# Delta rule in a two-layer kernel: the recurrence parts of the first two chunks move one slot earlier

## The reference, cut to what matters

```python
h = rmsnorm(layernorm(x))
q, k, v = (causal_conv_silu(h @ W, conv) for W, conv in ...)   # width 4 along the tokens
q, k = l2norm(q) * Kd ** -0.5, l2norm(k)
g = -exp(A_log) * softplus(h @ Wa + dt_bias);  beta = sigmoid(h @ Wb)
for each token:                                # S is 64 x 128 a head
    S = S * exp(g)
    delta = (v - k @ S) * beta
    S = S + outer(k, delta)
    o = q @ S
o = rmsnorm(o) * silu(h @ Wg)
x = x + o @ Wo
out = gelu(layernorm(x) @ W2 + b2) + x
```

## Time and profile before

| | |
|---|---|
| median of 3 runs | 4597.69 us (4597.64 to 4602.04) |
| the profiled execution | 4567.66 us, of it 4565.7 us span |
| TensorE busy | 3937.4 us (86%) |
| VectorE, ScalarE, GpSimd busy | 54%, 44%, 24% |
| delta rule, about | 2220 to 3960 us of the span |
| mean granted TensorE clock over the span | 0.927 |

### The profile page before, as it was taken

The page is one execution under the profiler, slowest core; times in us unless marked ns, Lnnn a source line. Parts: engine busy times, 40 slices in busy tenths (PEclk is TensorE's granted clock), DMA queues, the critical chain, the costliest instruction groups (busy, mean ns, idle before and its releaser), DMA issues. The chain is left out here.

```text
span 4565.7 us, 72621 instructions
## 1 busy us (share of the span) xinstructions
PE 3937.4 (86%) x23860; PEld 3048.4 (67%) x23860; DVE 2462.8 (54%) x5456; ACT 1990.0 (44%) x4069; POOL 1089.9 (24%) x1689
## 2 busy tenths in 40 slices
PE   5888788598999999993788888888888888769998
PEld 3555555377888888881577666666767677646666
DVE  7888888552222222224577767777777776421111
ACT  5655655111222222212466666666666666432222
POOL 0111111102222222212333433333333332200000
PEclk8888889799999999996799999999999999879999
DMA  1010010245555555552111111111111110011111
GB/s 34 29 42 28 28 42 20 78 133 180 184 184 184 184 184 184 184 169 71 37 38 43 44 37 42 43 42 43 42 43 43 42 43 24 20 51 55 55 55 46
DMA packets 220428, 345.93 MB, mean 76 GB/s; under 512 B 99956, under 2 KB 171380, under 8 KB 201972
## 3 DMA queue, kind: packets, MB, share of 16 engines
q1 hardware_dynamic: 196404, 271.69, 18.7%
q0 software_dynamic: 23760, 71.07, 4.9%
HBM read 275.56 MB, written 67.63 MB: 75 GB/s over the span
## 5 line engine op out<-in xcount | busy, mean ns | idle before, releaser
L525 ACT ACTIVATE moe_rel<-moe_fc 128x512 f32<-128x512 f32 x284 | 169.6, 597 | 799.6 <-PE moe_fc L490 799.6
L490 PE MATMUL moe_fc<-moe_xT,moe_win 128*128 128x256 f32 x2272 | 505.0, 381 | 1.5 <-issue 0.8
L501 PE MATMUL moe_o<-moe_wout,moe_hT 128*128 128x256 f32 x2272 | 502.0, 379 | 0.0
L490 PEld LDWEIGHTS moe_fc<-moe_xT,moe_win 128*128 128x128 f32 x2272 | 433.5, 191 | 61.5 <-issue 2.1
L501 PEld LDWEIGHTS moe_o<-moe_wout,moe_hT 128*128 128x128 f32 x2272 | 426.3, 190 | 55.1
L549 DVE TENSOR_TENSOR moe_hT<-moe_rel 128x512 f32<-128x512 f32 x284 | 196.7, 693 | 362.0 <-ACT moe_rel L525 362.0
L1777 DVE SCALAR_TENSOR_TENSOR gdr_y<-gdr_bank,gdr_cw,gdr_y 128x511 f32<-128x511 f32 (+2 forms) x384 | 287.5, 749 | 81.2 <-ACT gdr_y L2045 61.5
L2252 PE MATMUL gdr_bank<-gdr_hT,gdr_wqkv 128*128 128x512 f32 x512 | 260.4, 633 | 41.3 <-ACT gdr_qk L2060 24.7
L558 DVE COPY moe_osb<-moe_o 128x512 f32<-128x512 f32 x71 | 49.1, 692 | 424.9 <-PE moe_o L501 424.9
L723 DVE TENSOR_TENSOR ffn_z<-ffn_o,ffn_xres 128x512 f32<-128x512 f32 x32 | 20.6, 686 | 381.2 <-PE ffn_o L690 381.2
L690 PE MATMUL ffn_o<-ffn_wout,ffn_hT 128*128 128x256 f32 x1024 | 225.2, 381 | 0.0
(11 more groups left out here) (391 smaller groups left out, 8398.3 us busy)
## 6 DMA issues: line engine op xcount, KB each, us to landing
moe_win<-in_moe_w SPq DMA_DIRECT2D x71, 1024.0 KB, 8.0
moe_wout<-in_moe_w SPq DMA_DIRECT2D x71, 1024.0 KB, 5.2
slots_out<-moe_osb POOLq DMA_DIRECT2D x71, 256.0 KB, 7.5
ffn_xin<-mixed_rows SPq DMA_DIRECT2D x17, 512.0 KB, 3.8
gla_xp<-in_xT_rows SPq DMA_DIRECT2D x16, 512.0 KB, 4.7
gla_xres<-in_x_rows SPq DMA_DIRECT2D x16, 512.0 KB, 3.9
token_rows<-gla_x POOLq DMA_DIRECT2D x16, 512.0 KB, 3.4
rt_W<-in_fc_b SPq DMA_DIRECT2D x32, 256.0 KB, 3.3
```

The costliest lines, as they stand in the source:

```text
L490: ins = nc.tensor.matmul(fc_ps[j][:, m % 2, :], win[u][:, c, m * P:(m + 1) * P], xT[:, c, :], start=(c == 0), stop=(c == DT - 1))
L501: ins = nc.tensor.matmul(o_ps[u][:, t, :], hT[u][:, k, t * P:(t + 1) * P], wout[u][:, k, :], start=(k == 0), stop=(k == FT - 1))
L525: nc.scalar.activation(rel[:, j, :, :], fc_ps[j][:], ACT.Relu).then_inc(relu_done, 1)
```

## The change

Every part of chunks 0 and 1 goes one slot forward: slots 8 to 13 in place of 9 to 14, on all three engines. The squares of their outputs on ScalarE (`squares`, L2117) go from slots 12 and 15 to 11 and 14. On TensorE the block of `chunk(0, ...)` and `chunk(1, ...)` is put behind the key products in the code, so that in slot 8 the key products of the second pair come first; the wait for the scans (`DT`) moves to slot 8 with it. Nothing is added or taken away.

```diff
 CHUNK_AT = {0: (2, 0), 1: (2, 1), 2: (2, 2), 3: (3, 0), 4: (3, 1), 5: (3, 2),
-            9: (0, 0), 10: (0, 1), 11: (0, 2), 12: (1, 0), 13: (1, 1), 14: (1, 2)}
+            8: (0, 0), 9: (0, 1), 10: (0, 2), 11: (1, 0), 12: (1, 1), 13: (1, 2)}
...
-                        if here and slot in (12, 15):
-                            squares(0 if slot == 12 else 1, b)
+                        if here and slot in (11, 14):
+                            squares(0 if slot == 11 else 1, b)
...
-                        if t is not None and t < 2 and here:
-                            if slot == 9:
-                                pe.wait_ge(s["DT"], b * TT + TT)
-                            chunk(t, part, b, u)
                         if here and lv < 0:
                             if slot == 0 and past:
                                 pe.wait_ge(s["Uf"], b * TT)
                             if slot == 0 and end:
                                 pe.wait_ge(s["yb"], (b - 1) * 2)
                             key_products(pair, b, u)
+                        if t is not None and t < 2 and here:
+                            if slot == 8:
+                                pe.wait_ge(s["DT"], b * TT + TT)
+                            chunk(t, part, b, u)
```

## The result

The changed kernel took **4694.61 us** (median of 4 runs, 4673.76 to 4707.93) against 4599.86 (4 runs, 4597.64 to 4604.44) for the kernel before: ratio **1.0195 [1.0165, 1.0224]**, slower. The forecast was 4600 with a range up to 4628, so it was wrong. The same change was run twice more beside the kernel before: 1.0154 [1.0125, 1.0183] and 1.0145 [1.0118, 1.0172]. The cost of the change is therefore about 1.5% (61 to 68 us); what the first comparison had beyond that is told apart further down.

What follows compares the result with a forecast made beforehand. TensorE sets the pace through its own work, stalls and the clock lost after stalls. Per period -1.7 + 1.8 = +0.1, about +2 over 14 periods, so 4570, plus 30 us profile-to-median difference: 4600 us, range 4573 to 4628.

Steps and rivals of the forecast that it cites:

- the walk: One period followed on TensorE, VectorE and ScalarE from slot 8 to slot 14: -1.7 us if the clock stays high.
- the XT wait: Slot 12: TensorE's stall for the XT copies shrinks from 2.42 us to 0.3, as the squares went to slot 11.
- The last step: After the start of `first_half(5, 3)` in slot 14, old and new order are the same and TensorE is dense.
- the mark: Start of `first_half(5, 3)` in slot 14, at 2973.08 before and 2971.4 predicted; if it moves, the period moves.
- two signs of being wrong: Prediction would be wrong if `mix_out(0)` is slow in most periods, or if `reach` does not wait.
- The mean clock of the stretch: Delta rule's mean clock, 0.94 before: above 0.96 was to show the clock holds, at or below 0.94 the rates last.
- What the clock takes back: Low clock after the three new stalls in slots 9, 10/11 and 13: together 1.8 us a period.
- stall for R: Slot 9: TensorE waits 3.2 us for VectorE's R; clock drops in 3 of 4 periods, 1.3 each, 1.0 on average.
- rates' stall: Slots 10 and 11: TensorE waits 2.0 us for the softplus chain; clock drops 1 in 4 at 1.2, 0.3.
- stall for U's copy: Slot 13, before `first_half(4, 3)`: stall grows from 1.2 to 2.5 us; clock drops 1 in 2 at 1.0, 0.5.
- every new stall drops the clock: Rival: all three new stalls punished every time, 2.1 + 1.7 + 1.0 - 1.7 = +3.1 a period, 4641 us; chance 0.06.
- rates last: Rival: `rates(1)` behind the state's update on VectorE, `mix_out(0)` not faster; +2.0 a period, 4626 us; chance 0.27.

Runs made afterwards that it cites:

- rates_first: The changed kernel with VectorE's rates and scaled keys of slot 10 put ahead of the state's update: 4647.45 us, ratio 1.0153 to the kernel before.
- warm_half: The changed kernel with four spare unread matmuls in slot 9's wait for R and four in slot 13's wait for the U copy: 4597.52 us, 1.0042.
- chunk1_back: The changed kernel with chunk 1 back in slots 12 to 14 and its squares in 15, only chunk 0 moved: 4658.63 us, 1.0175.
- r_behind: The changed kernel with TensorE's chunk(0,1) of slot 9 put behind the rates and the first three turn_o: 4621.14 us, 1.0097.
- the third series: Runs on one chip with spare unread matmuls: three of the changed kernel (1.0123, 1.0183, 1.0187), one of the old kernel with chunk 0's squares in slot 11 (0.9938).
- the fifth: Series on another chip: the old kernel with chunk 0's squares at the end of slot 11 (4579.53 us, 0.9953), and the old kernel unaltered (4604.3, 1.0).
- before_2: The old kernel once more, unaltered: 4604.3 us, ratio 1.0.
- gather_late: The changed kernel with GpSimd's gathers for sequence b+2 held until the period's last merge is done: 4674.38 us, 1.0211.
- squares_back: The changed kernel with ScalarE's squares left in slots 12 and 15 as before: 4624.84 us, 1.0109.

## Why the prediction was wrong

**What held.** Each stall and each chain of the walk, in place and size: R 3.2 us (3.2 predicted), the rates 1.9 (2.0), U's copy 2.4 (2.5), `mix_out(0)` at the high clock (in 32 of 36 periods of the three profiles of the change), the XT wait down to 0.6 (0.3). Only the wait ahead of `mix_out(0)` is 1.0 and not 1.5, since TensorE comes late to it. From the start of `mix_out(0)` to that of `mix_out(1)` it took 10.4 us (10.1), from the end of `mix_out(1)` to `first_half(4, 3)` 8.2 (8.3). The last step, that behind the mark nothing changes, holds in the repeats: 16.4 to 16.5 us from the mark to the next period, 16.3 before. Neither of the two signs of being wrong that the prediction named came: `mix_out(0)` is fast in most periods, and `reach` waits. The mean clock of the stretch, at or below 0.94, was to point at the rates; it points at drops of the clock elsewhere.

**What failed is the step "What the clock takes back".** It took 1.8 us a period and should have taken 6.6 (the mark at 50.2, walked 43.6):

| term | priced | measured | from |
|---|---|---|---|
| stall for R | 1.0 (3 in 4 at 1.3) | 2.8 | `mix_out(0)` at 17.2, walked 14.4 |
| rates' stall | 0.3 (1 in 4 at 1.2) | 0.5 | rest of the 3.3 by which `mix_out(1)` ends late |
| stall for U's copy | 0.5 (1 in 2 at 1.0) | 3.4 | 10.5 from `first_half(4, 3)` to the mark, walked 7.1 |
| TensorE's lateness hidden in slots 12 and 13 | 0 | -0.1 | `first_half(4, 3)` 3.2 late behind 3.3 |

The difference of 4.8 a period, 14 times, is 67 us. Three errors are in it.

- I read single old stalls, one with a drop and one without, as a coin, while the drop came in nearly every period: `mix_out(0)` started at 16.5 or later in 23 of 24 periods of the two repeats, and all 24 were slow at the end. The profile of the kernel before had shares to read it from. In each of its 12 periods the stall of 3.16 us is followed by a slow `mix_out(0)` (5.2 to 6.6 us), and in 8 of the 12 the stall of 2.42 us is followed by a first product of level 4 (L2375) of 1.8 us in place of 1.0. I had followed one period, which had the longest `mix_out(0)` but one; from the mean old mark, 45.1, the walk gains 1.5 us and not 1.7.
- I priced a drop by the instruction that happened to stand behind the old stall (2.7 for one `mix_out`), but the low clock goes on through whatever follows, 7 to 9 us of dense work in the period shown.
- I let ScalarE's copies hide half of it, though their inputs, the `turn_o` results, come from the slowed TensorE: `rates` and three `turn_o` took 3.0 us longer than priced (3.42 and 2.80 against 1.85 and 1.4), and 2.8 of it arrived at `mix_out(0)`.

The third, largest term had been bounded at 1.5. The rival "every new stall drops the clock" had the mechanism nearly right, at a chance of 0.06. But its prices (2.1, 1.7 and 1.0) were too small where it mattered and came to +3.1 a period and 4641, where +5.1 was measured; by the prediction's own upper bounds (2.7, 1.7 and 1.5) it would have been +4.2. Its price for the rates' stall was too large: only in 6 of the 24 periods of the repeats is `mix_out(0)` or `mix_out(1)` at the low clock.

The Trainium skill (TensorE: Matmul & The Clock Gate, Part 1, on what is actually happening) was weighed there for a free-running window, from which the prediction drew that the same stall is punished or not by where it falls. The traces agree that equal stalls fare differently: in `rates_first` a wait of 2.25 us at one place of the period is followed by the low clock in some periods and by the high one in others. But the shares can't be taken from that, nor from the length of the stall. The wait for U's copy was punished in 24 of 24 periods of the repeats, in 10 of 12 of the change's first profile (waits of 1.7 and 1.8 us in the other two) and in 6 of 12 of `rates_first`. In `rates_first` the outcome goes with what TensorE did before, the length of `mix_out(1)`, but what decides it in a given period no run here tests.

That the clock is the cause, and not merely beside it, is shown by warm_half: with the stalls filled, the walked times come at both places, 14.4 to the start of `mix_out(0)` and 7.1 from `first_half(4, 3)` to the mark. 42 of the 61 us come back; the other 18 or 19 are still lost, most of them ahead of `first_half(4, 3)`, and for those the cause is read from the low clock in the rows there, not tested. That chunk 0's move brings in the stalls for R and for the rates is shown by chunk1_back; that the stall ahead of `rates` costs time, by r_behind.

**The rival "rates last"** had its mechanism wrong: `mix_out(0)` was fast, and taking the wait away (rates_first) gave nothing, since S came last in its place. That the time came out slower, as it said, is luck.

**The rest of the 95 us.** The first profile of the change has something that the repeats lack: VectorE and ScalarE start late in slot 15, and the profile names no instruction that held them:

```profile
3034.23 0.59 ACT L2141 COPY gdr_U<-gdr_bank 128x512 f32<-128x512 f32 x1 [8.12 <-remote]
...
3034.23 0.69 DVE L1932 TENSOR_TENSOR gdr_x<-gdr_bank,gdr_b 128x512 f32<-128x512 f32 x1 [1.68 <-remote]
```

```profile
3035.36 0.87 PE L2389 MATMUL gdr_bank<-gdr_U,gdr_Y 128*64 128x64 f32 x6 [5.13 <-ACT gdr_Y L2143]
```

From the mark to the next period it took 19.2 us, 16.4 in the repeats. This isn't of the change. Waits of this kind are in every trace taken where the old kernel's median was near 4600 (the first comparison, the third series and the fifth), in the old kernel's own too, profiled at 4603.92 (before_2):

```profile
DVE gdr_U L1870 <- remote: 51.9, 15, 5.3
...
ACT gdr_hT L2040 <- remote: 39.9, 11, 6.1
```

and in no trace of the series where it was near 4575, nor in the first profile of the old kernel (4567.66), 30 us below its median; the profile that the prediction used was of the lower level. They come while GpSimd gathers the next rows, but gathers moved by a few us (gather_late) are no test of them, as that series had none. At this level the old kernel is 21 to 27 us slower, the changed one 52 to 55 (4694.61 against 4642.37 and 4640.0), so 27 to 34 of the 95 us go with the level and not with the clock's price. Since each series was on another chip, the level may belong to the chip; no chip of the five was used twice, so that isn't tested. What sets the level, and why the change suffers more, stays open.

## What to carry to other kernels

A stall of 2 to 3 us in front of dense matmuls must be priced by what the clock does to all the work behind it, until the next wait that hides it; here stalls of 3.2 and 2.25 us cost another 2.8 and 3.4. How often the drop comes is counted over all periods of the old trace, not guessed from one. Before moving a dependent product to the head of TensorE's queue, look whether independent work can stand in front of it; where none can, a few unread matmuls, about as long as the stall, gave back 42 of 61 us. Read where the next bound is before paying for one: the filling in the old kernel cost the 0.7% that had just been gained, while moving one ScalarE block of four squares by a slot's edge gained 0.5 to 0.7%.

## What the runs showed of the hardware

- The low clock outlives its stall: windows of fully busy TensorE at a granted clock of 0.50, up to 7 us behind a stall of 3.2 us and 9 us behind one of 2.25.
- Equal stalls don't fare equally: behind a wait of 2.25 us at the same place of one profile (rates_first) the same 16 records took 1.95 us in one period and 2.99 in another. Behind waits of 1.9 us there the whole stretch took 9.5 to 9.8, while in squares_back, with waits of at most 1.9 and 1.1, it took 7.1 to 8.4 in 10 of 12 periods.
- Eight unread records in a stall of 3.2 us took 2 us of TensorE, and `rates` behind them took 1.85 us instead of 3.42.
- The same program has two levels, medians of 4571 to 4579 and of 4600 to 4604 us, that last through a whole series on one chip; the upper one goes with starts of ScalarE and VectorE up to 8 us late, without a releaser in the trace, in the slot in which GpSimd gathers.
